# Second phase of an attention + int8-FFN kernel: the residual add is done by accumulating DMAs into the output, and VectorE scales each fourth tile

## What is computed

```python
x = x + attn(layernorm(x), qkv_w, qkv_b, out_w, out_b)
# ffn of h = layernorm(x), h as rows of 512:
x_scale = max(abs(h).max() / 127, 1e-5)          # one scale for all rows
x_int8  = clip(round(h / x_scale), -128, 127)
out     = (x_int8 @ weight_int8.T) * x_scale * weight_scale.T + bias
x = x + out
```

## Time and profile before

| | before |
|---|---|
| median of three runs | 1138.6 us |
| profiled execution, its own time | 1139.31 us |
| its span in the trace | 1137.5 us |
| first phase | 0 to about 1033 us |
| setting the scale | 1033 to about 1040 us |
| tiles of the second phase | 1040 us to the end |
| busy in the whole span: TensorE / VectorE / ScalarE / GpSimd | 95% / 70% / 61% / 77% |

### The profile page before, as it was taken

One profiled execution on the slowest core, in us unless ns is written; L12 is line 12 of the kernel. 1 busy time (PEld: TensorE's weight loads), 2 busy tenths in 40 slices (PEclk: granted clock), 3 DMA queues, 4 the chain that ended last, 5 costly groups with the idle time before them and its releaser, 6 DMA issues. The chain is left out here.

```text
span 1137.5 us, 30783 instructions
## 1 busy us (share of the span) xinstructions
PE 1076.4 (95%) x11592; PEld 793.4 (70%) x11604; DVE 798.0 (70%) x1529; ACT 697.2 (61%) x1249; POOL 880.1 (77%) x1088
## 2 busy tenths in 40 slices
PE   2889999999999999999999999999999999965998
PEld 0567777778777777777777777777777777632443
DVE  5545767776776777767767767677766777766887
ACT  3566665666565666666666656666666666515996
POOL 4457787888778888888788878888788888842999
PEclk7899999999999999999999999999999999987999
DMA  7222333333333333333333333333333332421994
GB/s 259 56 57 56 88 87 92 87 87 90 89 91 87 89 94 95 94 86 86 92 85 94 81 94 87 85 90 89 90 89 87 90 90 58 131 78 51 376 356 186
DMA packets 73926, 120.80 MB, mean 106 GB/s; under 512 B 16433, under 2 KB 16945, under 8 KB 73778
## 3 DMA queue, kind: packets, MB, share of 16 engines
q1 hardware_dynamic: 72144, 116.98, 35.1%
q10 hardware_dynamic: 1634, 1.85, 0.6%
HBM read 36.97 MB, written 31.46 MB: 60 GB/s over the span
## 5 line engine op out<-in xcount | busy, mean ns | idle before, releaser
L534 PE MATMUL unit<-xt_hi,w_hi 128*128 128x256 f16 x1000 | 275.2, 275 | 12.3 <-DVE w_lo L1122 7.9
L534 PE MATMUL unit<-xt_hi,w_lo 128*128 128x256 f16 x1000 | 275.2, 275 | 0.0
L534 PE MATMUL unit<-xt_lo,w_hi 128*128 128x256 f16 x1000 | 275.1, 275 | 0.0
L785 ACT ACTIVATE relu<-unit,qk_bias_scaled 128x256 f32<-128x256 f32 x250 | 117.9, 472 | 186.1 <-PE unit L534 186.1
L1010 DVE SCALAR_TENSOR_TENSOR x_ring<-sc,x_ring 128x512 f16<-128x512 f32 x256 | 175.3, 686 | 56.2 <-ACT x_ring L827 52.5
L414 POOL TENSOR_TENSOR qk_lo<-f_t,qk_hi 128x512 f16<-128x512 f32 x128 | 149.4, 1167 | 55.8 <-ACT qk_hi L804 55.6
L827 ACT ACTIVATE x_ring<-sc 128x512 f16<-128x512 f32 x256 | 147.8, 591 | 67.3 <-PE sc L580 67.3
L431 POOL TENSOR_SCALAR_AFFINE_SELECT x_ring<-x_ring 128x512 f16<-128x512 f16 x256 | 164.2, 642 | 30.7 <-DVE x_ring L1010 24.2
L433 POOL TENSOR_SCALAR_AFFINE_SELECT x_ring<-x_ring 128x512 f16<-128x512 f16 x256 | 168.4, 658 | 0.0
L534 PEld LDWEIGHTS unit<-xt_hi,w_hi 128*128 128x128 f16 x1000 | 98.7, 99 | 31.8 <-DVE w_lo L1122 8.8
L534 PEld LDWEIGHTS unit<-xt_lo,w_hi 128*128 128x128 f16 x1000 | 98.7, 99 | 18.0 <-issue 0.3
(11 more groups left out here) (200 smaller groups left out, 2732.5 us busy)
## 6 DMA issues: line engine op xcount, KB each, us to landing
stack<-qk_hi SPq DMA_DIRECT2D x504, 64.0 KB, 2.0
xs<-x SPq DMA_DIRECT2D x64, 256.0 KB, 2.7
stack<-qk_lo SPq DMA_DIRECT2D x256, 64.0 KB, 2.0
out<-res SPq DMA_DIRECT2D x64, 256.0 KB, 3.7
x_spill<-xs SPq DMA_DIRECT2D x56, 256.0 KB, 2.3
x_ring<-x_spill SPq DMA_DIRECT2D x56, 256.0 KB, 4.2
stack<-qkv_wt SPq DMA_DIRECT2D x4, 768.0 KB, 11.4
x_ring<-out_wt SPq DMA_DIRECT2D x1, 1024.0 KB, 5.1
```

Source lines behind the costliest of these rows:

```text
L534: mm = pe.matmul(dst[:, 0:GT], wp[:, k, f:f + P], xp[:, g % 2, k, :], start=(n == 0), stop=(n == len(terms) - 1))
L785: act.activation(relu[:, i % 4, :], src[:, 0:GT], ACT.Relu, bias=qk_bias_scaled[:, f:f + 1]).then_inc(qk_done, 1)
```

## The change

There is no scratch tensor any more. The first phase writes x1 of each tile straight to its place in the output, for all 64 tiles (the last 8 as well), and loads come from there. In the second phase GpSimd computes nothing. It issues, for each tile, a DMA that adds `y` to the output rows in HBM (`accum_op=ALU.add`), after it has once waited for all stores of the first phase. `y` becomes a ring of 8, and `scale_back` waits for the landing of the accumulating DMA of 8 tiles before. SP only loads x1, each tile as soon as the tile 16 before it is quantised. VectorE does the work of `scale_tile` itself for tiles 3, 7, 11 and so on, right ahead of their `quantise`, and waits for its own result. ScalarE skips these tiles and reads its scales straight from `affine`, without the copy to `cur`.

```diff
-    x1_spill = nc.dram_tensor("x1_spill", (N, P, E), F32, kind="Internal").ap()
...
-                def store_x1(c):
-                    if not 0 <= c < N - CB:
+                def store_x1(c, upto_chunk=N - CB):
+                    if not 0 <= c < upto_chunk:
                         return
 
                     sp.wait_ge(x1_ready, upto(c))
-                    sp.dma_start(x1_spill[c], xs[:, c % CB, :]).then_inc(x1_stored[c % CB], 16)
+                    sp.dma_start(out_t[c], xs[:, c % CB, :]).then_inc(x1_stored[c % CB], 16)
...
+                for t in range(RING // 2):
+                    load_x1(t)
+                for c in range(N - CB, N - 3):
+                    store_x1(c, N)
+
+                sp.wait_ge(o_ready, upto(N - 1, 2))
+                for t in range(RING // 2, RING):
+                    load_x1(t)
+                for c in range(N - 3, N):
+                    store_x1(c, N)
                 for c in range(CB):
-                    sp.wait_ge(x1_stored[c], 16 * (B - 1))
+                    sp.wait_ge(x1_stored[c], 16 * B)
...
+            Y_DEEP = 8
+            OWN_EVERY = 4
...
                 def reload(i, t):
 
-                    sp.dma_start(x1[t], x1_spill[i * RING + t]).then_inc(x1_loaded[t], 16)
...
+                    sp.wait_ge(xq_ready, seen(i - 1, t))
+                    sp.dma_start(x1[t], out_t[i * RING + t]).then_inc(x1_loaded[t], 16)
...
-                    pool.tensor_tensor(res[:, t % RING, :], y[:, t % DEEP, :], tile_x1(t, last), ALU.add).then_inc(res_ready, 1)
...
+                def add_to_output(i, t):
+
                     pool.wait_ge(y_ready, seen(i, t))
+                    pool.dma_start(out_t[i * RING + t], y[:, (i * RING + t) % Y_DEEP, :], accum_op=ALU.add).then_inc(added[t], 16)
...
                 def quantise(i, t, first):
 
-                    dve.wait_ge(u_ready, seen(i, t))
+                    if scaled_by_vector(t):
+
+                        wait_x1(dve, i, t, i == ROUNDS - 1)
+                        dve.tensor_scalar(u[:, t % DEEP, :], tile_x1(t, i == ROUNDS - 1), affine[:, i, 0, t:t + 1], affine[:, i, 1, t:t + 1],
+                                          ALU.mult, ALU.add).then_inc(own_ready, 1)
+                        dve.wait_ge(own_ready, (i * RING + t) // OWN_EVERY + 1)
+                    else:
+
+                        dve.wait_ge(u_ready, scaled(i, t))
...
-                    if not (first and t < DEEP):
-
-                        dve.wait_ge(res_ready, seen(i, t - DEEP))
-                    dve.tensor_tensor(y[:, t % DEEP, :], acc[t % DEEP][:, :], dq[:, :], ALU.mult).then_inc(y_ready, 1)
+                    k = i * RING + t
+                    if k >= Y_DEEP:
+
+                        dve.wait_ge(added[(k - Y_DEEP) % RING], ((k - Y_DEEP) // RING + 1) * 16)
+                    dve.tensor_tensor(y[:, k % Y_DEEP, :], acc[t % DEEP][:, :], dq[:, :], ALU.mult).then_inc(y_ready, 1)
```

More of the change, by code:

```diff
@@ L363, in _, with load_x1 @@
                     stack_part(g + 2, 0, 0)
[L365 to L369, removed]
+                def load_x1(t):
+                    sp.dma_start(x1[t], out_t[t]).then_inc(x1_loaded[t], 16)
+                for t in range(RING // 2):
[7 more added lines that the diff above has]
+                    store_x1(c, N)
                 for c in range(CB):
-                    sp.wait_ge(x1_stored[c], 16 * (B - 1))
+                    sp.wait_ge(x1_stored[c], 16 * B)
             @block.gpsimd
@@ L1261, in build @@
             affine = buf(two, "affine", [P, ROUNDS, 2, RING])
-            cur = buf(two, "cur", [P, 2, RING])
             dq = buf(two, "dq", [P, E])
@@ L1271, in build @@
             xq_t = buf(two, "xq_t", [P, DEEP, EC, P], BF16)
-            y = buf(two, "y", [P, DEEP, E])
-            res = buf(two, "res", [P, RING, E])
+            y = buf(two, "y", [P, Y_DEEP, E])
             tp = [two.enter_context(nc.psum_tensor(f"tp{i}", [P, 2 * EC, P], BF16)) for i in range(DEEP)]
             acc = [two.enter_context(nc.psum_tensor(f"acc{i}", [P, E], F32)) for i in range(DEEP)]
-            res_stored = [sem(f"res_stored{i}") for i in range(RING)]
+            added = [sem(f"added{i}") for i in range(RING)]
             step2 = sem("step2")
@@ L1283, in build @@
             dq_ready = sem("dq_ready")
-            cur_ready = sem("cur_ready")
             u_ready = sem("u_ready")
+            own_ready = sem("own_ready")
             xq_ready = sem("xq_ready")
@@ L1291, in build, with scaled_by_vector, scaled @@
             y_ready = sem("y_ready")
-            res_ready = sem("res_ready")
             block2 = two.enter_context(nc.Block())
+            def scaled_by_vector(t):
+                return t % OWN_EVERY == OWN_EVERY - 1
+            def scaled(i, t):
+                return sum(not scaled_by_vector(n) for n in range(i * RING + t + 1))
             def rounds(eng, body):
@@ L1312, in _ @@
             def _(sp):
-                def store(i, t):
-                    sp.wait_ge(res_ready, seen(i, t))
-                    sp.dma_start(out_t[i * RING + t], res[:, t % RING, :]).then_inc(res_stored[t % RING], 16)
                 def reload(i, t):
-                    sp.dma_start(x1[t], x1_spill[i * RING + t]).then_inc(x1_loaded[t], 16)
[L1323 to L1333, removed]
+                    sp.wait_ge(xq_ready, seen(i - 1, t))
+                    sp.dma_start(x1[t], out_t[i * RING + t]).then_inc(x1_loaded[t], 16)
+                for i in range(1, ROUNDS):
+                    for t in range(RING if i < ROUNDS - 1 else RING - CB):
+                        reload(i, t)
+                for s in added:
                     sp.wait_ge(s, 16 * ROUNDS)
@@ L1337, in _ @@
             def _(pool):
-                def add_residual(i, t, first, last):
-                    wait_x1(pool, i, t, last)
+                def add_to_output(i, t):
                     pool.wait_ge(y_ready, seen(i, t))
-                    if not first:
-                        pool.wait_ge(res_stored[t % RING], i * 16)
-                    pool.tensor_tensor(res[:, t % RING, :], y[:, t % DEEP, :], tile_x1(t, last), ALU.add).then_inc(res_ready, 1)
-                def body(i, first, last):
+                    pool.dma_start(out_t[i * RING + t], y[:, (i * RING + t) % Y_DEEP, :], accum_op=ALU.add).then_inc(added[t], 16)
+                for c in range(CB):
+                    pool.wait_ge(x1_stored[c], 16 * B)
+                for i in range(ROUNDS):
                     for t in range(RING):
-                        add_residual(i, t, first, last)
-                rounds(pool, body)
+                        add_to_output(i, t)
             @block2.tensor
@@ L1399, in _, with scale_tile @@
                 act.wait_ge(affine_ready, 2)
-                def fetch(i, first):
-                    if first:
+                def scale_tile(i, t, first, last):
+                    if scaled_by_vector(t):
                         return
[L1405 to L1410, removed]
                     wait_x1(act, i, t, last)
@@ L1415, in scale_tile @@
                         act.wait_ge(xq_ready, seen(i, t - DEEP))
-                    own = affine[:, 0] if first else cur
-                    act.activation(u[:, t % DEEP, :], tile_x1(t, last), ACT.Identity, bias=own[:, 1, t:t + 1],
-                                   scale=own[:, 0, t:t + 1]).then_inc(u_ready, 1)
+                    act.activation(u[:, t % DEEP, :], tile_x1(t, last), ACT.Identity, bias=affine[:, i, 1, t:t + 1],
+                                   scale=affine[:, i, 0, t:t + 1]).then_inc(u_ready, 1)
                 def turn_out(i, t, first):
@@ L1430, in body @@
                 def body(i, first, last):
-                    fetch(i, first)
                     for t in range(RING):
```

## The result

The changed kernel takes 1162.5 us in the median of four runs (1159.72 to 1163.12), against 1138.7 before: a ratio of 1.0207, 95% interval 1.0187 to 1.0228, 2.1% slower. The prediction was 1168 us, with 1137 to 1200 as its range.

A forecast was written before the change was run, and what follows sets the result against it. DMA engines were to bind: 64 accumulations x 1.44 plus 40 loads x 0.76 give 122.6 us; less 3.0 for early loads, from 1045.2, plus 2.0 landing, span 1166.8; with 1.1 added, 1168 us, range 1137 to 1200.

The forecast's parts named there:

- The first phase at nothing: First phase: eight new stores late in SP's queue delay the barrier by 0; with the longest landing, 0.5 us.
- Quantise falls to 0.43: Second phase, VectorE: without GpSimd's add, quantise falls from 0.66 to 0.43 us.
- VectorE's scaling, 0.52 on the loop, pace 1.435: Second phase: scaling each fourth tile before its quantise takes 0.52 us on the loop, giving a compute pace of 1.435 us.
- the pair (add away, scaling in): Second-phase compute alone: GpSimd's add removed and VectorE's scaling added come to 0.9 us slower, called a wash.
- The loop as what holds 1.42: Old second phase: TensorE and VectorE's scale-back and quantise form a 2.84 us loop over two tiles, 1.42 per tile.
- An accumulation is 0.68 + 0.76 = 1.44, a load 0.76: DMA engines, second phase: an accumulation costs a store's read plus a load's read, 1.44 us; a load costs 0.76.
- My own lower figure: DMA engines at the fast rate: 0.64 us per transfer, 1.28 per accumulation, 107.5 us in all; 1153 us predicted.
- The rest of the sum: Second phase: early loads 3.0 us, first accumulation issued 0.4 after its y, last landing 2.0; span 1166.8 us.
- The dearer one: Rival: accumulations cost more than two reads, through GpSimd's issuing or a third engine pass; 1172 to 1211 us, chance 0.20.
- The hidden ones: Rivals with cheap HBM read, compute binding: no change, 1137 to 1141 us, 0.14; shorter VectorE scaling, 1134 to 1136, 0.14.
- The signs: Second phase: scale-backs wait from about tile ten, pace near 2.2 then 1.44 us, landing over 8, quantise 0.43.

The follow-up runs named there:

- plain copies: The changed kernel with GpSimd's DMAs as plain copies in place of accumulations, second residual left out: 1141.56 us, ratio 1.0033 to the kernel before.
- the loop open: The kernel before, with VectorE scaling back tile t-4 instead of t-3 behind the quantise of tile t (BACK = 4): 1138.43 us, ratio 1.0003.
- the three transfers: The changed kernel with GpSimd's DMAs as plain copies and SP loading one more 256 KB tile of input per tile: 1157.12 us, ratio 1.0169.
- the half-precision y: The changed kernel with y in float16, widened by the accumulating DMA as it adds: 1148.01 us, ratio 1.0085.
- the first of the two spread mixtures: Accumulating DMAs for each eighth of tiles 0-39, two of three of 40-60; GpSimd adds the others; ScalarE scales all, BACK = 4: 1135.69 us, ratio 0.998.

## Why the prediction was right, and where its numbers were off

**The first phase at nothing.** Right: the barrier passes 0.33 us after the statistics, with eight more stores ahead of it.

**Quantise falls to 0.43.** 0.418.

**VectorE's scaling, 0.52 on the loop, pace 1.435.** It took 0.57 from start to start (1071.51 to 1072.08; the record is 0.54), and three tiles of 1.30 with one of 1.88 are 1.445. Exposed it costs 8.8 us against leaving it with ScalarE, and it was wrong of me to call the pair (add away, scaling in) a wash without naming what lies beside it: 1.30 for all tiles was to be had, because ScalarE manages 1.30, not the 1.40 that its records sum to. The net of compute alone came out near what I had: with plain copies the last `y` is done 102.2 us after the barrier's statistics, before it was 100.5, so 1.6 more where the step had 0.9. The other 2.2 of the 3.8 us by which that kernel is slower lie behind the last `y` (6.38 us in place of 4.14).

**The loop as what holds 1.42.** Half right. It does hold it, but VectorE's slow quantise and GpSimd's add beside it hold it as well: with the loop open both are busy all the time, at 1.42. I had read GpSimd's 20.00 of 20 in the earlier trace rows and then set it aside. For the change that makes no difference, since it removes both.

**An accumulation is 0.68 + 0.76 = 1.44, a load 0.76.** The mechanism held, by the copies, the three transfers and the half-precision y. The size was off: 1.285 and 0.715, so 64 x 1.285 + 40 x 0.715 = 110.8 us in place of 122.6. The mis-sized term is the engines' rate. I took share 1 as full, at 371 GB/s, and the kernel before was asking for no more than that; three plain transfers a tile went at 408. My own lower figure, 0.64 from the first loads, was the right one, and the sum with it is 107.5, under the measured 110.8 mostly by the 0.07 us that a load and an accumulation cost together beyond three plain transfers, 40 times. The Trainium skill's rule that a reduction moves at about half the rate of a copy ("Collectives: The Full Stack", section "The bandwidth ceiling: the fold count and why AG ≠ RS ≠ AR") is stated for the steps of ring collectives; for these DMAs this case's traces agree with it: 1.285 against 0.642 us, a factor of 2.0.

**The rest of the sum.** The measured second phase was 128.0 us long where the sum had 134.0 (1032.8 to 1166.8): 11.8 less for the rate; 1.3 more for the end (3.3 after the last bytes at 1154.6, I had 2.0); 1.2 more for the first accumulation, which GpSimd has issued by 1043.4, 1.7 us after its `y`, where I had 0.4; about 2.0 more because the engines ran at 162 to 194 GB/s from 1043 to 1049 before both queues were filled. That leaves 1.3 us unexplained. The 6.0 us together turn the 1168 into 1162, against 1162.5 measured. That the forecast came within 5.5 us is in part luck: one term was 11.8 too large, and 5.8 of that is made good by what I had left out or made too small, with the unexplained rest.

**The rivals.** The dearer one fell: GpSimd issues in 0.86 us and no third pass shows. The hidden ones fell with the read of HBM. The sign of the whole lay in one question, whether the second read takes engine time, and no row of before could answer it.

**The signs.** The pace was 2.00 and then 1.445, landing over 8 us, quantise at 0.42. The waits for landing began with the scale-back of tile 15 rather than the tenth.

## What to carry to other kernels

An accumulating DMA moves work from a compute engine to the DMA engines at the price of two plain transfers. Where these already run at 90% of what they can do (371 of 408 GB/s here), price it first, by time and not by the bytes that the trace counts. Used for 14 of the 64 tiles, where the windows showed room, and with ScalarE scaling all tiles and the loop opened, it came out 0.4% faster than the kernel before. And before moving an operation to another engine look what stands behind it in order there: 0.54 us of scaling cost 0.58 per use because it stood in the one gap on which TensorE waits.

## What the runs showed of the hardware that was not expected

- The trace's bytes leave out what an accumulation reads at its destination: 262 GB/s counted is 393 moved, counting that read once more, at a share of 1.10.
- A DMA share of 1.0 isn't a measure of how much room is left: it was 1.02 at 371 GB/s, 1.04 at 408, and 1.13 for accumulations alone.
- Where GpSimd's queue has the last transfers, 3.2 to 4.2 us pass from the last bytes to the end of the span (3.3 in the changed kernel, 4.2 with plain copies; the 3.8 to 4.3 of the expectation above was read from coarser windows), against 0.9 in the kernel before and 0.7 to 1.3 in the other kernels with SP last. The time follows, by 3.2 us of the medians (1132.75 to 1129.53). What GpSimd's queue does in them no row shows.
- GpSimd needs 0.54 us to issue a plain copy of 128 rows and 0.86 for an accumulation, and VectorE's quantise beside it stays at 0.42. "SBUF — State Buffer" of the Trainium skill (section "🔬 SBUF: two separate sides") has VectorE's two-port forms lock GpSimd out while it writes descriptors; if they did so here, it cost neither of them a time that these rows show: the last four issues, with no quantise beside them, take 0.86 to 0.88 us too. GpSimd's adds are another matter. In the first of the two spread mixtures three quantises took 1.31, 1.84 and 1.48 us, and each ends 0.28 or 0.29 us after the add that GpSimd was making beside it (at 1108.80, 1111.81 and 1118.68).
